# Opening of a one-core Perceiver kernel: spare products on TensorE, key weights split in three parts, and another order of TensorE's and ScalarE's first work

## The chip, the cores and the metric

The kernel runs on one core of a Trainium2 chip. A core has TensorE (PE in the profile: matmuls, with their weight loads listed apart as PEld), VectorE (DVE), ScalarE (ACT), GpSimd (POOL), SyncE (SP, which here only issues transfers) and 16 DMA engines. The engines run their own programs in order and meet through semaphores. The metric is the device time of one execution in microseconds (us), lower is better.

## The reference, cut to what matters

128 query rows of width 256 pass two layers. The change touches only the first operation of the first layer, a cross-attention over a context of 12544 rows with 16 heads, whose keys are 64 wide and whose values are 16 wide:

```python
q = (layernorm(x) @ wq)       # 128 x 1024, 16 heads of 64
k = (ctx @ wk)                # 12544 x 1024
v = (ctx @ wv)                # 12544 x 256, 16 heads of 16
attn = softmax(q @ k.T / sqrt(64), axis=-1)   # per head
x = x + attn @ v
```

After it come self-attention, a gated feed-forward, a second cross-attention, a causal self-attention and a mixture of experts. None of their code is changed.

## The kernel before, in words

**Tiles.** The context comes transposed, in chunks of 512 columns; the first one, the tail, has 256 (`TAIL_TILES` = 2). A chunk's keys are made in eight pairs of heads `p`. Context and key weights are each split into a high and a low part (`ctxT_hi`, `ctxT_lo`, `wk_hi`, `wk_lo`), and a pair's keys are six products, `TERMS` = 6, three for each half of the contraction (`key_term`, L361). The high part is a copy by ScalarE, the low part a subtraction by VectorE (weights) or GpSimd (context). Scores are made in eight steps `t`; a step takes 32 queries of a group of four pairs, so steps 0 to 3 need pairs 0 to 3 and the first half of the queries, steps 4 to 7 need pairs 4 to 7 and the second half (`scores`, L384). For each step VectorE takes the extreme value (`maxima`, L619), ScalarE the exponentials (`exponentials`, L554) followed by a drain that signals `scores_read`, VectorE transposes them (L638), and TensorE multiplies by the values (`weighted`, L394).

**The opening**, before the first call of `chunk`, is written out by hand, engine by engine. TensorE: the layer norm's transposes, then for each half of the heads: the queries (`queries`, L376; 8 matmuls, which the trace shows as 16 records, since a matmul of this type is recorded twice), a wait for the key weights of that half (`wk_split`), the tail's keys of four pairs in PSUM banks 4 and 5 alternately, and a wait for the scaled queries; after the first half also score steps 0 and 1. ScalarE: the context's high part, the copy of the normed x, the high part of the first 512 key weights columns (`wk_hi`, L581), the scaling of the queries (`keep_queries`, L548), four key copies (`keep_keys`, L544), the high parts of the second half of the key weights (L586) and of the value weights (L588), exponentials of step 0, second queries, key copies 4 and 5, exponentials of step 1, key copies 6 and 7, the next chunk's context (L540). VectorE takes the low parts of the key weights in two halves (L723) and of the value weights (L726), then the maxima.

**After it** comes `chunk(0, ...)`: score steps 2 and 3 of the tail, its values (L368), steps 4 and 5 (each waits until ScalarE has read the bank two steps before, `scores_read`), and the next chunk's keys. The first transfers are all issued at the start: x, the two halves of wq and the first full chunk by SyncE, the tail, the two halves of wk, and wv by ScalarE's queue.

**Spare products** (`spare_products`, L284) are matmuls of the identity with itself into a bank that nobody reads; the kernel has them already in the later stages, none in the opening.

Of the kernel before, what the change touches and what calls it, by code (L numbers as in the profile page):

```python
# [16 lines left out]
BANK = 512  # L17
# [5 lines left out]
TAIL_TILES = (N_KEYS // P) % CHUNK_TILES  # L23
# [257 lines left out]
def spare_products(pe, m, bank, count):  # L281

    for _ in range(count):
        pe.matmul(m.bank(bank)[:, 0:P], m.ident[:, :], m.ident[:, :], start=True, stop=True, skip_group_check=True)  # L284


def layer_norm_tensor(pe, m, s, n, bank):
    pe.wait_ge(s["xn_ready"], n("xn_ready"))
    for k in range(DK):
        t = pe.transpose(m.bank(bank)[:, k * P:(k + 1) * P], m.xn[:, k * P:(k + 1) * P], m.ident[:, :])  # L290
    t.then_inc(s["xnT_full"], 1)


def layer_norm_scalar(act, m, s, n, bank):
    act.wait_ge(s["xnT_full"], n("xnT_full"))
    act.copy(m.xnT[:, :, :], m.bank(bank)[:, 0:D].rearrange("p (k c) -> p k c", c=P)).then_inc(s["xnT_ready"], 1)
# [48 lines left out]


LAST_HALF, LAST_SUM = 3, 4


def per_head(t, f, u):  # L350
# [4 lines left out]
def xattn0_tensor(pe, m, s, n):  # L355
    def key_term(slot, p, nt, bank, i):

        k, term = divmod(i, 3)
        w = (m.wk_hi, m.wk_hi, m.wk_lo)[term]
        c = (m.c_hi, m.c_lo, m.c_hi)[term][slot]  # L360
        return pe.matmul(m.bank(bank)[:, 0:nt * P], w[:, k, p * P:(p + 1) * P], c[:, k, 0:nt * P],  # L361
                         start=(i == 0), stop=(i == TERMS - 1))
# [8 lines left out]
    def queries(half):  # L371
        pe.wait_ge(s[f"wq{half}"], 16)
        for i in range(4):
            p = 4 * half + i
            for k in range(DK):
                t = pe.matmul(m.bank(6 + half)[:, i * P:(i + 1) * P], m.wq[:, k, p * P:(p + 1) * P], m.xnT[:, k, :],  # L376
                              start=(k == 0), stop=(k == DK - 1))
        t.then_inc(s["q_full"], 1)

    def scores(slot, t, nt):  # L380
        group, qs = t // 4, slice(t % 4 * 32, t % 4 * 32 + 32)
        for j in range(4):
            for odd, rows in enumerate((TOP, LOW)):
                i = pe.matmul(m.ps[32 * j:32 * (j + 1), 2 * (t % 2) + odd, 0:nt * P], m.qT[rows, 4 * group + j, qs],  # L384
                              m.keys[slot][rows, 4 * group + j, 0:nt * P], start=True, stop=True,
                              skip_group_check=True)
        i.then_inc(s["scores_full"], 1)
# [115 lines left out]
        i.then_inc(s["last_turned"], 1)  # L503

    pe.wait_ge(s["ident"], 1)
    layer_norm_tensor(pe, m, s, n, 3)
    pe.wait_ge(s["xnT_ready"], n("xnT_ready"))
    for half in range(2):
        queries(half)
        if half == 0:  # L510
            pe.wait_ge(s["ctx_split"], n("ctx_split", 2))
            pe.sem_inc(s["raw_free"], 1)
        pe.wait_ge(s["wk_split"], n("wk_split"))
        for p in range(4 * half, 4 * half + 4):
            if p % 4 >= 2:
                pe.wait_ge(s["k_kept"], n("k_kept"))
            for i in range(TERMS):
                done = key_term(0, p, TAIL_TILES, 4 + p % 2, i)
            done.then_inc(s["k_full"], 1)
        pe.wait_ge(s["q_ready"], n("q_ready"))  # L520
        if half == 0:
            pe.wait_ge(s["k_kept"], n("k_kept", 2))
            for t in range(2):
                scores(0, t, TAIL_TILES)
    pe.wait_ge(s["wv_split"], n("wv_split"))
    chunk(0, TAIL_TILES, 0, 2)
    chunk(1, CHUNK_TILES, TAIL_TILES, 2)
# [8 lines left out]
def xattn0_scalar(act, m, s, n):  # L536
    def split_context(slot, k, nt):
        if k == 0:
            act.wait_ge(s[f"raw{slot}"], n(f"raw{slot}", 16))
        act.copy(m.c_hi[slot][:, k, 0:nt * P], m.raw[slot][:, k, 0:nt * P]).then_inc(s["ctx_hi"], 1)  # L540

    def keep_keys(slot, p, nt):
        act.wait_ge(s["k_full"], n("k_full"))
        act.copy(m.keys[slot][:, p, 0:nt * P], m.bank(4 + p % 2)[:, 0:nt * P]).then_inc(s["k_kept"], 1)  # L544

    def keep_queries(half):
        act.wait_ge(s["q_full"], n("q_full"))
        act.mul(m.qT[:, 4 * half:4 * half + 4, :], m.bank(6 + half).rearrange("p (h c) -> p h c", c=P),  # L548
                -float(X0_DK) ** -0.5).then_inc(s["q_ready"], 1)

    def exponentials(slot, t, nt, between=None):
        act.wait_ge(s["max_ready"], n("max_ready"))
        for odd in range(2):
            i = act.activation(m.probs[t % 2][:, odd, 0:nt * P], m.ps[:, 2 * (t % 2) + odd, 0:nt * P], ACT.Exp,  # L554
                               bias=m.peak[slot][:, 1, 2 * (t // 4) + odd, t % 4:t % 4 + 1], scale=-1.0,
                               accum_out=m.totals[slot][:, 1, 2 * (t // 4) + odd, t % 4:t % 4 + 1])
            if odd == 0 and between:
                keep_keys(*between, CHUNK_TILES)
        i.then_inc(s["probs_ready"], 1)
        act.drain().then_inc(s["scores_read"], 1)  # L560

    def chunk(slot, nt, ahead, first=False):
        for t in range(2 if first else 0, STEPS):
            keys = 1 - slot if t > 1 else slot
            kept = t < 2 or ahead
            exponentials(slot, t, nt, (keys, KEEP_BETWEEN[t]) if kept and t in KEEP_BETWEEN else None)
            if t == STEPS - 1:
                act.wait_ge(s["below_ready"], n("below_ready"))
                act.activation(m.shrink[slot][:, :, :, :], m.below[:, :, :, :],
                               ACT.Exp).then_inc(s["alpha_ready" if ahead else "alpha_last"], 1)  # L570
            if kept:
                for p in KEEP_AFTER.get(t, ()):
                    keep_keys(keys, p, CHUNK_TILES)
            if ahead > 1 and t in SPLIT_STEPS:
                split_context(slot, SPLIT_STEPS.index(t), CHUNK_TILES)

    for k in range(DK):
        split_context(0, k, TAIL_TILES)
    layer_norm_scalar(act, m, s, n, 3)
    act.wait_ge(s["wk0"], 16)  # L580
    act.copy(m.wk_hi[:, :, 0:BANK], m.wk[:, :, 0:BANK]).then_inc(s["wk_hi"], 1)  # L581
    keep_queries(0)
    for p in range(4):
        keep_keys(0, p, TAIL_TILES)
    act.wait_ge(s["wk1"], 16)
    act.copy(m.wk_hi[:, :, BANK:2 * BANK], m.wk[:, :, BANK:2 * BANK]).then_inc(s["wk_hi"], 1)  # L586
    act.wait_ge(s["wv"], 16)
    act.copy(m.wv_hi[:, :, :], m.wv[:, :, :]).then_inc(s["wv_hi"], 1)  # L588
    exponentials(0, 0, TAIL_TILES)
    keep_queries(1)  # L590
    for p in range(4, 6):
        keep_keys(0, p, TAIL_TILES)
    exponentials(0, 1, TAIL_TILES)
    for p in range(6, 8):
        keep_keys(0, p, TAIL_TILES)
    for k in range(DK):
        split_context(1, k, CHUNK_TILES)
    chunk(0, TAIL_TILES, 2, first=True)
    chunk(1, CHUNK_TILES, 2)
    looped = ("raw0", "raw1", "k_full", "max_ready", "below_ready")  # L600
    n.restart(act, s, *looped)
    with act.Fori(0, (N_FULL - 4) // 2):
        chunk(0, CHUNK_TILES, 2)
        chunk(1, CHUNK_TILES, 2)
        n.restart(act, s, *looped)
    chunk(0, CHUNK_TILES, 2)
    chunk(1, CHUNK_TILES, 1)
    chunk(0, CHUNK_TILES, 0)
    act.wait_ge(s["last_full"], 1)
    act.copy(m.last_out[0:64, :, :], m.ps[0:64, 6:8, 0:P]).then_inc(s["last_kept"], 1)  # L610
    act.wait_ge(s["last_full"], 2)
    act.copy(m.last_two[:, :, :], m.ps[:, 6:8, P:2 * P]).then_inc(s["last_kept"], 1)


def xattn0_vector(dv, m, s, n):
# [101 lines left out]

    dv.wait_ge(s["x"], 16)
    layer_norm_vector(dv, m, s, n, m.x[0][:, :])
    for half in range(2):  # L720
        cols = slice(half * BANK, (half + 1) * BANK)
        dv.wait_ge(s["wk_hi"], n("wk_hi"))
        dv.tensor_tensor(m.wk_lo[:, :, cols], m.wk[:, :, cols], m.wk_hi[:, :, cols],  # L723
                         ALU.subtract).then_inc(s["wk_split"], 1)
# [949 lines left out]
def build(nc, a, out):  # L1674
# [3 lines left out]
    with nc.Block() as block:  # L1678
        @block.tensor
        def tensor_program(pe):  # L1680
            n = Counts()
            xattn0_tensor(pe, m, s, n)
            attn0_tensor(pe, m, s, n)
            ffn0_tensor(pe, m, s, n)
            xattn1_tensor(pe, m, s, n)
            attn1_tensor(pe, m, s, n)
            moe_tensor(pe, m, s, n)
# [122 lines left out]
```

## Time and profile before

| | |
|---|---|
| time, median of 3 executions | 977.41 us (976.40 to 977.99) |
| time of the profiled execution | 980.61 us |
| its span in the trace | 978.0 us |
| TensorE busy | 951.1 us (97%) |
| VectorE, ScalarE, GpSimd busy | 71%, 60%, 38% |
| first cross-attention | from the start to about 650 us |
| opening, until the next chunk's keys start | 26.28 us |

The span runs from the first to the last instruction; 2.6 us of the profiled execution's time lie around it. Times in the trace are counted from the span's start. A matmul's end is modelled and neighbours overlap, so starts say more than ends.

### The profile page before, as it was taken

How to read it: one execution, taken by the hardware profiler on the slowest of the kernel's cores; microseconds unless marked ns; L12 is line 12 of the kernel's file. 1: busy time of each engine (PE TensorE's matmuls, PEld its weight loads, DVE VectorE, ACT ScalarE, POOL GpSimd, SP SyncE). 2: the span in 40 equal slices, each digit the busy share in tenths (PEclk: the TensorE clock that was granted, in tenths of full speed). 3: DMA queues.
4: the chain of work that ended last, by engine and by line, in shares of the span. 5: the costliest groups of instructions: out<-in, count | busy, mean ns of one | idle time of the engine just before them, and what ended most of it. 6: DMA issues, size and time to landing. Idle time of an engine off the chain costs nothing.

```text
span 978.0 us, 30798 instructions
## 1 busy us (share of the span) xinstructions
PE 951.1 (97%) x13287; PEld 703.0 (72%) x13287; DVE 689.9 (71%) x870; ACT 587.4 (60%) x1405; POOL 373.1 (38%) x407
## 2 busy tenths in 40 slices
PE   6999999999999999999999999988989999999998
PEld 6666666666666666666666666678978877789998
DVE  3788888888888888888888888763035654367886
ACT  5677766666666676666666666633246663336664
POOL 2344444444444444444444343331023334213332
PEclk9999999999999999999999999998999999999999
DMA  6100000100100001000100100049648988408992
GB/s 221 26 24 23 25 24 24 25 24 24 25 24 24 25 24 24 24 25 24 25 24 24 24 3 3 3 153 393 216 174 263 284 275 283 152 1 284 323 338 95
DMA packets 78296, 97.80 MB, mean 100 GB/s; under 512 B 21585, under 2 KB 56673, under 8 KB 78177
## 3 DMA queue, kind: packets, MB, share of 16 engines
q1 hardware_dynamic: 77088, 94.40, 29.9%
q8 instruction: 104, 1.70, 0.7%
q10 hardware_dynamic: 1088, 1.57, 0.4%
q14 instruction: 16, 0.12, 0.0%
HBM read 95.42 MB, written 0.13 MB: 98 GB/s over the span
## 4 chain that ended last, share of the span: by engine, by line
PE 89%; issue 4%; DVE 2%; POOL 2%; DMA 2%; ACT 1%; SPq 0%; ACTq 0%; DVEq 0%; POOLq 0%
PE ps L361 29%; PE ps L384 18%; PE ps L394 9%; PE ps L368 7%; PE ps L1508 6%; PE ps L1109 3%; PE ps L1010 3%; PE ps L1525 2%; PE ps L1529 2%; PE ps L1526 2%; PE ps L1098 1%; DMA m_shared_w<-in_m_sw 1%; PE ps L1100 1%; POOL m_w_lo L1490 1%; PE ps L1099 1%
## 5 line engine op out<-in xcount | busy, mean ns | idle before, releaser
L554 ACT ACTIVATE probs<-ps,x_peak 128x512 f32<-128x512 f32 (+1 forms) x400 | 269.6, 678 | 178.2 <-DVE x_peak L619 167.5
L619 DVE TENSOR_REDUCE x_peak<-ps 128x2 f32<-128x1024 f32 (+1 forms) x200 | 237.2, 1186 | 93.8 <-PE ps L384 93.8
L638 DVE STREAM_TRANSPOSE probsT<-probs 128x1024 f32<-128x1024 f32 (+1 forms) x200 | 242.9, 1215 | 13.2 <-ACT probs L554 12.6
L384 PE MATMUL ps<-keys,qT 64*32 64x512 f32 (+1 forms) x3200 | 195.7, 584 | 2.7 <-ACTq L560 1.6
L361 PE MATMUL ps<-ctxT_hi,wk_hi 128*128 128x512 f32 (+1 forms) x400 | 163.1, 408 | 0.8 <-ACT keys L544 0.8
L361 PE MATMUL ps<-ctxT_lo,wk_hi 128*128 128x512 f32 (+1 forms) x400 | 155.1, 388 | 0.0
L800 POOL TENSOR_SCALAR vals<-vals_t,x_side 128x512 f32<-128x512 f32 (+1 forms) x100 | 152.1, 1539 | 7.2 <-POOL x_totals L789 3.9
L361 PE MATMUL ps<-ctxT_hi,wk_lo 128*128 128x512 f32 (+1 forms) x400 | 154.1, 385 | 0.0
L361 PEld LDWEIGHTS ps<-ctxT_hi,wk_hi 128*128 128x128 f32 x400 | 75.3, 188 | 73.7 <-issue 39.8
L544 ACT COPY keys<-ps 128x512 f32<-128x512 f32 (+1 forms) x200 | 110.4, 577 | 28.7 <-PE ps L361 20.8
L766 POOL TENSOR_TENSOR ctxT_lo<-ctx_raw,ctxT_hi 128x512 fp32r<-128x512 f32 x48 | 61.6, 1284 | 134.7 <-ACT ctxT_hi L540 134.5
L384 PEld LDWEIGHTS ps<-keys,qT 64*32 64x32 f32 x3200 | 58.8, 106 | 70.6 <-issue 52.6
L394 PE MATMUL ps<-probsT,vals 64*32 64x128 f32 x6144 | 100.5, 271 | 0.0
L394 PEld LDWEIGHTS ps<-probsT,vals 64*32 64x32 f32 x6144 | 87.0, 105 | 18.2 <-issue 18.0
L361 PEld LDWEIGHTS ps<-ctxT_hi,wk_lo 128*128 128x128 f32 x400 | 75.6, 189 | 15.7
L361 PEld LDWEIGHTS ps<-ctxT_lo,wk_hi 128*128 128x128 f32 x400 | 75.7, 189 | 12.4
L554 ACT ACTIVATION_READ_ACCUMULATOR probs<-ps,x_peak 128x1 f32 x400 | 78.6, 197 | 0.0
L1290 POOL TENSOR_TENSOR c1T_lo<-ctx_two,c1T_hi 128x512 fp32r<-128x512 f32 (+1 forms) x25 | 31.3, 1251 | 93.4 <-ACT c1T_hi L1171 93.4
L783 POOL TENSOR_TENSOR x_parts<-x_totals,x_shrink 128x32 f32<-128x32 f32 x24 | 6.1, 253 | 158.6 <-DMA x_shrinkT<-x_shrink 158.6
L1480 POOL TENSOR_TENSOR m_w_lo<-m_w,m_w_hi 128x1024 fp32r<-128x1024 f32 x15 | 35.4, 2362 | 72.0 <-ACT m_w_hi L1557 72.0
L1508 PE MATMUL ps<-xnT,m_w 128*128 128x128 f32 x512 | 59.9, 275 | 0.0
L1508 PEld LDWEIGHTS ps<-xnT,m_w 128*128 128x128 f32 x512 | 58.6, 192 | 0.3 <-issue 0.3
(258 smaller groups left out, 1310.0 us busy)
## 6 DMA issues: line engine op xcount, KB each, us to landing
m_w<-in_m_w SPq DMA_DIRECT2D x32, 1024.0 KB, 7.8
ctx_raw<-in_ctxT SPq DMA_DIRECT2D x24, 512.0 KB, 3.7
ctx_two<-in_ctxT SPq DMA_DIRECT2D x24, 512.0 KB, 4.2
ctx_one<-in_ctx SPq DMA_DIRECT2D x24, 512.0 KB, 5.5
x_shrinkT<-x_shrink SPq DMA_DIRECT2D x384, 1.0 KB, 1.7
f_h1T<-in_f_h1T SPq DMA_DIRECT2D x1, 4096.0 KB, 18.5
f_h2T<-in_f_h2T SPq DMA_DIRECT2D x1, 4096.0 KB, 28.2
m_shared_w<-in_m_sw SPq DMA_DIRECT2D x2, 1024.0 KB, 8.9
```

What stands on the lines that cost most here:

```text
L361: return pe.matmul(m.bank(bank)[:, 0:nt * P], w[:, k, p * P:(p + 1) * P], c[:, k, 0:nt * P], start=(i == 0), stop=(i == TERMS - 1))
L368: return pe.matmul(m.bank(4 + half)[:, 0:nt * P], w[:, k, half * P:(half + 1) * P], c[:, k, 0:nt * P], start=(i == 0), stop=(i == TERMS - 1))
L384: i = pe.matmul(m.ps[32 * j:32 * (j + 1), 2 * (t % 2) + odd, 0:nt * P], m.qT[rows, 4 * group + j, qs], m.keys[slot][rows, 4 * group + j, 0 ...
L394: i = pe.matmul(m.ps[32 * c:32 * (c + 1), 6 + two, 0:P], m.vals[slot][rows, b, c, :], m.probsT[slot][rows, c, b, :], start=(b == 0), stop= ...
L544: act.copy(m.keys[slot][:, p, 0:nt * P], m.bank(4 + p % 2)[:, 0:nt * P]).then_inc(s["k_kept"], 1)
L554: i = act.activation(m.probs[t % 2][:, odd, 0:nt * P], m.ps[:, 2 * (t % 2) + odd, 0:nt * P], ACT.Exp, bias=m.peak[slot][:, 1, 2 * (t // 4) ...
L619: dv.tensor_reduce(m.peak[slot][:, 1, cs, t % 4], m.ps[:, 2 * (t % 2):2 * (t % 2) + 2, 0:nt * P], AX.X, ALU.min).then_inc(s["dve" if t == ...
L638: i = dv.transpose(m.probsT[slot][:, cs, 0:4 * nt, t % 4 * 32:t % 4 * 32 + 32], m.probs[t % 2][:, :, 0:nt * P].rearrange("p c (b k) -> p c ...
L766: gp.tensor_tensor(m.c_lo[slot][:, k, 0:nt * P], m.raw[slot][:, k, 0:nt * P], m.c_hi[slot][:, k, 0:nt * P], ALU.subtract).then_inc(s["ctx_ ...
L800: t = gp.tensor_scalar(m.vals[slot][:, 0:4 * nt, cs, side * X0_DV:(side + 1) * X0_DV], m.vals_t[slot][:, 0:4 * nt, cs, :], m.side[:, side: ...
L1480: eng.tensor_tensor(m.w2_lo[c % 2][:, os, :], second_weights(m, c)[:, os, :], m.w2_hi[c % 2][:, os, :], ALU.subtract).then_inc(s[f"m_w2_lo ...
L1508: t = pe.matmul(m.bank(2 * (c % 2) + half)[:, i * P:(i + 1) * P], w1[:, k, o * P:(o + 1) * P], m.xnT[:, k, :], start=(k == 0), stop=(k == ...
```

## The change: what it does

It edits the opening in four places. Seven spare products into bank 7 stand ahead of the layer norm's transposes, behind the wait for the identity. The key weights are split in three parts, columns 0 to 255, 256 to 511 and 512 to 1023, by ScalarE and VectorE alike, and TensorE waits for a part ahead of pairs 0, 2 and 4. TensorE makes the second half of the queries ahead of score steps 0 and 1, and its wait for the first scaled queries and for the four key copies moves with these. ScalarE splits the third part of the weights between key copies 1 and 2; it scales the second queries and copies key pair 4 ahead of the exponentials of step 0, and key pair 5 ahead of those of step 1.

```diff
+WK_PARTS = slice(0, BANK // 2), slice(BANK // 2, BANK), slice(BANK, 2 * BANK)
@@ xattn0_tensor
     pe.wait_ge(s["ident"], 1)
+    spare_products(pe, m, 7, 7)
     layer_norm_tensor(pe, m, s, n, 3)
     pe.wait_ge(s["xnT_ready"], n("xnT_ready"))
     for half in range(2):
...
         if half == 0:
             pe.wait_ge(s["ctx_split"], n("ctx_split", 2))
             pe.sem_inc(s["raw_free"], 1)
-        pe.wait_ge(s["wk_split"], n("wk_split"))
+        else:
+            pe.wait_ge(s["q_ready"], n("q_ready"))
+            pe.wait_ge(s["k_kept"], n("k_kept", 2))
+            for t in range(2):
+                scores(0, t, TAIL_TILES)
         for p in range(4 * half, 4 * half + 4):
+            if p in (0, 2, 4):
+                pe.wait_ge(s["wk_split"], n("wk_split"))
             if p % 4 >= 2:
                 pe.wait_ge(s["k_kept"], n("k_kept"))
             for i in range(TERMS):
                 done = key_term(0, p, TAIL_TILES, 4 + p % 2, i)
             done.then_inc(s["k_full"], 1)
-        pe.wait_ge(s["q_ready"], n("q_ready"))
-        if half == 0:
-            pe.wait_ge(s["k_kept"], n("k_kept", 2))
-            for t in range(2):
-                scores(0, t, TAIL_TILES)
+    pe.wait_ge(s["q_ready"], n("q_ready"))
     pe.wait_ge(s["wv_split"], n("wv_split"))
@@ xattn0_scalar
     act.wait_ge(s["wk0"], 16)
-    act.copy(m.wk_hi[:, :, 0:BANK], m.wk[:, :, 0:BANK]).then_inc(s["wk_hi"], 1)
+    for cols in WK_PARTS[0:2]:
+        act.copy(m.wk_hi[:, :, cols], m.wk[:, :, cols]).then_inc(s["wk_hi"], 1)
     keep_queries(0)
-    for p in range(4):
+    for p in range(2):
         keep_keys(0, p, TAIL_TILES)
     act.wait_ge(s["wk1"], 16)
-    act.copy(m.wk_hi[:, :, BANK:2 * BANK], m.wk[:, :, BANK:2 * BANK]).then_inc(s["wk_hi"], 1)
+    act.copy(m.wk_hi[:, :, WK_PARTS[2]], m.wk[:, :, WK_PARTS[2]]).then_inc(s["wk_hi"], 1)
+    for p in range(2, 4):
+        keep_keys(0, p, TAIL_TILES)
     act.wait_ge(s["wv"], 16)
     act.copy(m.wv_hi[:, :, :], m.wv[:, :, :]).then_inc(s["wv_hi"], 1)
+    keep_queries(1)
+    keep_keys(0, 4, TAIL_TILES)
     exponentials(0, 0, TAIL_TILES)
-    keep_queries(1)
-    for p in range(4, 6):
-        keep_keys(0, p, TAIL_TILES)
+    keep_keys(0, 5, TAIL_TILES)
     exponentials(0, 1, TAIL_TILES)
@@ xattn0_vector
-    for half in range(2):
-        cols = slice(half * BANK, (half + 1) * BANK)
+    for cols in WK_PARTS:
         dv.wait_ge(s["wk_hi"], n("wk_hi"))
         dv.tensor_tensor(m.wk_lo[:, :, cols], m.wk[:, :, cols], m.wk_hi[:, :, cols],
                          ALU.subtract).then_inc(s["wk_split"], 1)
```

## Rows read from the trace of the kernel before

**Rows 1.** The page: busy time, share of the span and instructions.

```profile
PE 951.1 (97%) x13287; PEld 703.0 (72%) x13287; DVE 689.9 (71%) x870; ACT 587.4 (60%) x1405; POOL 373.1 (38%) x407
```

**Rows 2.** Stretches: length, each engine's busy time, PEclk (granted clock), DMA share, GB/s.

```profile
0.00:26.28 26.28, 18.23 (x190) 15.21 (x190) 9.77 (x17) 13.85 (x35) 7.75 (x29) 1.00 0.59 206
26.28:649.75 623.47, 620.70 (x10752) 404.19 (x10752) 503.69 (x518) 417.69 (x1048) 276.56 (x314) 1.00 0.09 21
```

**Rows 3.** The chain that ended last, in the opening: start, us, what.

```profile
14.76 0.95 ACT wk_hi L586
```

**Rows 4.** Timeline of TensorE: start, us, engine line op, count, idle before and releaser.

```profile
5.43 0.66 PE L290 MATMUL ps<-ident,xn 128*128 128x128 f32 x2 [5.43 <-DVE xn L306]
6.82 3.75 PE L376 MATMUL ps<-xnT,x_wq 128*128 128x128 f32 x16 [0.73 <-DMA x_wq<-in_x_wq]
...
11.22 0.41 PE L361 MATMUL ps<-ctxT_hi,wk_hi 128*128 128x256 f32 x1
11.43 0.41 PE L361 MATMUL ps<-ctxT_lo,wk_hi 128*128 128x256 f32 x1
...
14.90 1.10 PE L384 MATMUL ps<-keys,qT 64*32 64x256 f32 x32 [0.56 <-ACT keys L544]
15.93 2.05 PE L376 MATMUL ps<-xnT,x_wq 128*128 128x128 f32 x16
17.74 0.36 PE L361 MATMUL ps<-ctxT_hi,wk_hi 128*128 128x256 f32 x1
...
25.69 0.67 PE L384 MATMUL ps<-keys,qT 64*32 64x256 f32 x16 [0.49 <-ACTq L560]
```

**Rows 5.** Timeline of ScalarE.

```profile
8.05 1.04 ACT L581 CAST wk_hi<-x_wk 128x1024 fp32r<-128x1024 f32 x1 [1.55 <-DMA x_wk<-in_x_wk]
...
12.10 0.37 ACT L544 COPY keys<-ps 128x256 f32<-128x256 f32 x1 [0.88 <-PE ps L361]
...
15.60 0.62 ACT L588 CAST wv_hi<-x_wv 128x512 fp32r<-128x512 f32 x1
18.20 0.47 ACT L554 ACTIVATE probs<-ps,x_peak 128x256 f32<-128x256 f32 x1 [1.98 <-DVE x_peak L619]
...
19.34 0.60 ACT L548 ACTIVATE qT<-ps 128x512 f32<-128x512 f32 x1
...
22.26 1.14 ACT L540 CAST ctxT_hi<-ctx_raw 128x512 fp32r<-128x512 f32 x2
23.38 0.47 ACT L554 ACTIVATE probs<-ps,x_peak 128x256 f32<-128x256 f32 x1
```

**Rows 6.** Timeline of VectorE.

```profile
9.13 1.23 DVE L723 TENSOR_TENSOR wk_lo<-x_wk,wk_hi 128x1024 fp32r<-128x1024 f32 x1 [3.84 <-ACT wk_hi L581]
...
16.88 0.68 DVE L726 TENSOR_TENSOR wv_lo<-x_wv,wv_hi 128x512 fp32r<-128x512 f32 x1
...
22.65 0.69 DVE L619 TENSOR_REDUCE x_peak<-ps 128x2 f32<-128x512 f32 x1 [2.69 <-PE ps L384]
```

**Rows 7.** Timeline of GpSimd.

```profile
1.90 0.29 POOL L323 TENSOR_SCALAR_AFFINE_SELECT ident<-ident 128x128 f32<-128x128 f32 x1
```

**Rows 8.** Instructions of the tiles x_wk and x_wv: issue of transfers, and their landing.

```profile
L879 ACTq DMA_DIRECT2D x_wk<-in_x_wk x2: 487/489/491, 1.3 to 1.8; - x2
...
DMA to landing us min/median/max: 6.8/7.9/9.0
...
L880 ACTq DMA_DIRECT2D x_wv<-in_x_wv x1: 640/640/640, 2.3 to 2.3; - x1
...
DMA to landing us min/median/max: 9.9/9.9/9.9
```

**Rows 9.** Stretches after the cross-attention; the third value from the right is PEclk.

```profile
671.00:672.00 1.00, 1.00 (x7) 1.00 (x6) 0.00 (x0) 0.00 (x0) 0.00 (x0) 0.50 0.99 397
...
677.00:678.00 1.00, 1.00 (x7) 1.00 (x7) 0.93 (x3) 0.00 (x0) 0.00 (x0) 0.58 1.08 362
...
729.00:730.00 1.00, 0.70 (x4) 0.46 (x3) 0.75 (x2) 0.18 (x1) 0.38 (x1) 0.99 0.98 382
```

## The prediction, made blind

> **What bounds the kernel now.** I read the page first: TensorE is busy 97% of the span [rows 1]. A table of stretches then shows where its idle time is. From 26.28 us to 649.75 us it is idle for 2.8 us in 623 [rows 2], with no wait to gain from. In the first 26.28 us it is busy for 18.23 us only, so 8.05 us are idle. The opening is the one place the edit touches, and what it saves there moves the long busy stretch forward as a whole. I take as the marker the first scores of step 5, at 25.69 us [rows 4]: behind them TensorE runs without a gap. The question is how much earlier they start.
>
> The timelines show what holds them back. TensorE is first needed at 5.43, has nothing until 6.82 (it waits for wq), and then works slowly: 16 query records take from 6.82 to 10.41, about 0.22 us each, where the same 16 take from 15.93 to 17.74 later, 0.11 each; key products are 0.21 us apart at 11.22 and 11.43 [rows 4], and, counting six of them behind the start at 17.74, 0.12 there. A ratio of two is the ratio of TensorE's two levels, 1.2 and 2.4 GHz. The granted clock is listed as 1.00 for the whole opening [rows 2], which the spacing contradicts, so I go by the spacing: the low level lasts until the spacing halves, at about 12.2 us. The chain of waits passes from TensorE's key products to ScalarE's split of the second half of wk at 14.76 [rows 3], then VectorE, then exponentials, and ScalarE is last to release step 5.
>
> **The change part by part.** I follow the new program from event to event.
>
> *Spare products.* The identity is written at 2.19 [rows 7]. Seven matmuls are 14 records; at the slow query spacing (3.59/16 = 0.224) that is 3.1 us, 2.25 to 5.4. The normed x is there at 5.43, so the transposes lose nothing, and if they lose 0.1 us, the wait for wq until 6.8 (0.73 us idle [rows 4]) covers it; beyond some 0.2 us the cover would be gone, and each further tenth would be a tenth of the path. What they buy is an earlier rise. Before the rise at 12.2 TensorE had been steadily busy since 6.82, 5.4 us. Elsewhere it runs at half, 0.50, at 671 and comes back within 677 to 678, and a second half-clock stretch ends by 729 to 730 [rows 9]. With spares, work begins at 2.25. By 5.4 us of work the rise comes at 7.7, or 8.5 if the 0.8 us gap ahead of the queries doesn't count. At 7.7 four query records are slow and twelve fast: 0.9 + 1.4, so they end at about 9.1; with 8.5 at about 9.5; with a rise ahead of them, at 8.6.
>
> *First key weights in two parts.* wk's first half is there at 8.05. A ScalarE split of 512 elements is 0.62 [rows 5], a VectorE one 0.68 [rows 6]. Part 0 is ready at 8.05 + 0.62 + 0.68 + 0.05 of handing over = 9.4, where the whole was ready at 10.36 (9.13 + 1.23). Part 1 follows at 10.0, ahead of pair 2, so its extra fixed cost is hidden. Key products start at 9.43, where they started at 10.41: this needs both the split and the faster queries. Four pairs of six at 0.12 take 2.87 us, to 12.3. Pair 2 needs key copy 0 (ScalarE: pair 0 done at 10.33, copy 0.37, 10.70) and begins at 10.86; pair 3 needs copy 1 at 11.42 and begins at 11.58. No stall, but margins of 0.15 us.
>
> *Other queries first.* Before, TensorE stood 0.56 us for key copy 3 ahead of the scores [rows 4]; now the queries (1.81 us) fill this: 12.3 to 14.1. Scores of steps 0 and 1 take 1.03 (14.90 to 15.93): to 15.13. Queries moved ahead pass no transfer; wq's second half is not awaited in the old trace.
>
> *Third part of wk.* ScalarE reaches it after copy 1, at 11.35. The transfer lands at 1.8 + 9.0 = 10.8 [rows 8], 0.5 us of slack. Split to 12.4, VectorE (1.23) to 13.65, needed at 15.13. Key copies 2 and 3 are queued behind it: done at 12.97, needed at 14.1. wv lands at 2.3 + 9.9 = 12.2 [rows 8], its split runs 12.9 to 13.5. All hidden; the chain's 0.95 us at 14.76 is gone from the path.
>
> *Copies ahead of exponentials.* Pairs 4 and 5 run 15.13 to 16.64 and their results need 0.15 more. The maxima of step 0 are ready at 14.7 + 0.7 [rows 6] = 15.4, but ScalarE stands until key 4 arrives: copy 16.1 to 16.45. This is the added wait: the exponentials, and scores steps 2 and 3 behind them, are queued behind it for 0.9 us. Exponentials of step 0 take 1.14 (18.20 to 19.34 [rows 5]): to 17.5; copy 5 to 17.85; step 1 to 19.0; copies 6 and 7 0.74, to 19.75. TensorE stands some 0.6 us ahead of pair 7, until 17.95, and ends it at 18.7, so its step 2 and 3 scores and values are behind ScalarE, not ahead.
>
> *The sum.* ScalarE's split of the next context, which began at 22.26 [rows 5], begins at 19.75: 2.5 us earlier. From here both programs are the same: two splits 1.12, exponentials 2 and 3 2.3, step 5 on TensorE at 23.15 instead of 25.69. GpSimd's low part of the context moves along. I take 0.1 off for narrow handovers: **2.4 us gained**. On the profiled execution that is 980.61 - 2.4 = 978.2; it lies 3.2 us above the median of the timed ones, so on their scale 977.41 - 2.4 = **975.0 us**.
>
> Bounds. Without any effect of the spares, key products start at 10.41 at slow spacing, end at 14.2, queries to 16.0, scores to 17.05, pair 4 done at 17.95, exponentials 18.3 to 19.4 and 19.7 to 20.9, copies to 21.6: 0.7 us gained by the new order alone. At the other end a rise ahead of the queries gains nothing over 9.43, since the split bounds that; dropping all my handovers gives 2.9.
>
> The row shows a rise 5.4 us after steady work began, and less elsewhere [rows 9]. The Trainium skill, "TensorE: Matmul & The Clock Gate", in its part on the HAM clock gate, says that the point of the rise depends on how the first matmul falls against a free-running counter, and warns not to fit a specific number of cold matmuls. By the trace alone the gain is 2.4 us; by that page the same kernel would give anything from 0.7 to 2.4 from one execution to the next. No run so far shows which.
>
> **The rivals.**
>
> *The spares don't bring the rise forward* (22%). The 0.8 us gap between transposes and queries may make the count start anew at 6.82, as before, and the rise comes at 12.2: 0.7 us gained, 976.7 us. For it: TensorE was also busy at 5.43, and that did not count then. Against: the gap is short beside the work around it. The page's rule named above would put executions in this case too, a reason for its chance.
>
> *Given back behind the opening* (10%). If some other chain, through VectorE's maxima or GpSimd's context split, holds step 5 or the next keys, the gain is lost: 977.4 us. For it: VectorE has 503.69 us of work in 623 [rows 2], with little to spare to catch up. Against: in the long stretch TensorE never waits for it longer than 2.8 us in total.
>
> *Slower: the clock falls in the new gaps* (8%). The new program leaves TensorE idle at 17.4 to 17.95, briefly ahead of the values, then 0.5 us ahead of steps 4 and 5 each, about 1.8 us in 5.7. The half-clock stretch from 671 to 677.4 [rows 9] lasted 6.4 us. A stretch of that length in the busy part costs half of it, 3.2 us: 0.8 us slower, 978.2 us. It decides from 4.8 us on, half of which is the gain. Against: before, gaps of 0.56, about 0.8 and 0.49 us within 11 us had no such effect.
>
> **How the numbers follow.** The forecast has 60%, with its own range 974.3 to 975.8 (a gain of 1.6 to 3.1). About 0.2% or 2.0 us is what a measurement of this kernel can tell from no change, and the forecast lies just beyond it: I give 48 of its 60 to faster and 12 to the same. The first rival, the second, and half of the third fall within 0.2%. A delay beyond 2 us has 4%, nearly all from a longer fall of the clock, and 1% from the forecast's lucky side of the others goes to faster. Faster 49%, same 47%, slower 4%. The range of eight in ten runs from 973.9 (the upper bound on the gain, and the timed median's own scatter) to 977.2, which takes in the first rival and leaves out the other two.
>
> **What would show it.** In the trace after: 14 records of L284 from 2.25; query records 0.11 apart by 9 us; the first L361 at about 9.4; no fall behind L586's successor; ScalarE waiting for TensorE ahead of key copy 4; the next chunk's ScalarE context split at 19.75; keys of 512 columns from 23.7, no gap behind. Wrong would be: query records 0.22 apart until 10.4, a transfer of wk's second half landing beyond 12.4, spacing doubled anywhere between 17 and 30 us, or a TensorE idle time beyond 3 us between 26 and 650.

## The result, and the profile after

Over 22 executions of each, the changed kernel took 979.76 us (977.98 to 983.89) where the one before took 977.32 us. The ratio is 1.003, with an interval of 1.002 to 1.004: **0.3% slower**, where 2.4 us had been predicted as a gain. The opening did get shorter. The loss lies behind it, in code that the edit doesn't touch.

The page after: the span, the row of busy times and the queue that carries instructions. The last columns of the queue are packets, megabytes and share of the DMA engines.

```profile
span 981.0 us, 30828 instructions
...
PE 956.9 (98%) x13301; PEld 705.4 (72%) x13301; DVE 689.8 (70%) x871; ACT 586.9 (60%) x1406; POOL 373.1 (38%) x407
...
q8 instruction: 105, 1.72, 0.7%
```

TensorE is busy 5.8 us longer than in [rows 1], with 14 matmuls and 14 weight loads more. A matmul shown as busy includes time in which it stands. Before, q8 carried 104 packets and 1.70 MB: 1.70 MB over the two times 13287 records of TensorE in [rows 1] is some 64 bytes for each record, so that each counts as one instruction, and a packet of 16.4 KB holds about 256 of them.

The stretches after, which answer to [rows 2]:

```profile
0.00:25.06 25.06, 20.60 (x205) 17.30 (x205) 9.97 (x18) 13.69 (x36) 7.74 (x29) 1.00 0.63 216
25.06:649.75 624.69, 622.31 (x10684) 402.80 (x10680) 501.65 (x514) 416.49 (x1046) 276.46 (x314) 1.00 0.09 21
```

The next chunk's keys start at 25.06, 1.22 us ahead of 26.28 before. TensorE's timeline of the opening after, beside [rows 4]:

```profile
2.24 3.36 PE L284 MATMUL ps<-ident 128*128 128x128 f32 x14 [2.24 <-POOL ident L323]
5.59 0.69 PE L290 MATMUL ps<-ident,xn 128*128 128x128 f32 x2
7.56 3.58 PE L377 MATMUL ps<-xnT,x_wq 128*128 128x128 f32 x16 [1.28 <-DMA x_wq<-in_x_wq]
10.90 0.37 PE L362 MATMUL ps<-ctxT_hi,wk_hi 128*128 128x256 f32 x1
11.10 0.28 PE L362 MATMUL ps<-ctxT_lo,wk_hi 128*128 128x256 f32 x1
...
13.92 1.95 PE L377 MATMUL ps<-xnT,x_wq 128*128 128x128 f32 x16
15.79 1.09 PE L385 MATMUL ps<-keys,qT 64*32 64x256 f32 x32
...
19.66 0.39 PE L362 MATMUL ps<-ctxT_hi,wk_hi 128*128 128x256 f32 x1 [0.43 <-ACT keys L548]
...
24.46 0.67 PE L385 MATMUL ps<-keys,qT 64*32 64x256 f32 x16 [0.47 <-ACTq L564]
```

The spare products stand where they should, and the queries behind them are still slow: 16 records in 3.34 us. Keys are 0.20 apart once and then 0.12, the spacing that the prediction read behind the rise: the clock rises at about 10.9, not at 7.7. Step 5 starts at 24.46, 1.23 us ahead of before. ScalarE's timeline after, beside [rows 5]:

```profile
7.93 1.14 ACT L586 CAST wk_hi<-x_wk 128x512 fp32r<-128x512 f32 x2 [1.25 <-DMA x_wk<-in_x_wk]
...
12.87 1.05 ACT L591 CAST wk_hi<-x_wk 128x1024 fp32r<-128x1024 f32 x1
...
17.83 0.37 ACT L548 COPY keys<-ps 128x256 f32<-128x256 f32 x1 [1.33 <-PE ps L362]
18.09 0.48 ACT L558 ACTIVATE probs<-ps,x_peak 128x256 f32<-128x256 f32 x1
...
21.17 1.15 ACT L544 CAST ctxT_hi<-ctx_raw 128x512 fp32r<-128x512 f32 x2
```

The parts of the weights land and are split without a wait on the path, the added wait ahead of key copy 4 is there (1.33 us), and the context's split comes 1.09 us earlier than before.

**Where it is given back.** In each chunk of the loop ScalarE makes `x_shrink` once, so its starts tell how long a chunk takes. Two of them, in the kernel before:

```profile
160.53 0.23 ACT L569 ACTIVATE x_shrink<-x_below 128x32 f32<-128x32 f32 x1
186.13 0.23 ACT L569 ACTIVATE x_shrink<-x_below 128x32 f32<-128x32 f32 x1
```

and the same two after:

```profile
159.33 0.23 ACT L573 ACTIVATE x_shrink<-x_below 128x32 f32<-128x32 f32 x1
185.97 0.23 ACT L573 ACTIVATE x_shrink<-x_below 128x32 f32<-128x32 f32 x1
```

Before, the chunk takes 25.60 us; after, 26.64. Behind the first two, nearly every chunk of either kernel takes 25.60. Five of the changed kernel take 26.64, 26.88, 26.54, 26.87 and 26.34, which is 5.3 us more in all. Before has one of 26.97, near the end of the stage, and its last takes 25.33 against 24.65. From the first mark to the 25th: 613.17 us before, 616.33 after, 3.16 lost.

TensorE's timeline shows the lost microsecond of the first late chunk, after:

```profile
157.81 2.03 PE L395 MATMUL ps<-probsT,vals 64*32 64x128 f32 x128
159.59 3.00 PE L385 MATMUL ps<-keys,qT 64*32 64x512 f32 x32
162.52 0.50 PE L362 MATMUL ps<-ctxT_hi,wk_hi 128*128 128x512 f32 x1
```

It is busy without a gap, yet the 32 score records take 2.93 us until the next product. At the same place of the changed kernel without its spare products (first experiment) they take 1.90:

```profile
157.77 2.03 PE L395 MATMUL ps<-probsT,vals 64*32 64x128 f32 x128
159.54 1.98 PE L385 MATMUL ps<-keys,qT 64*32 64x512 f32 x32
161.44 0.50 PE L362 MATMUL ps<-ctxT_hi,wk_hi 128*128 128x512 f32 x1
```

No releaser is named, and the records are the same in number. What falls there is the transfer of one packet of instructions. The transfers of 157 to 163 us after, each slice 0.15 us:

```profile
GB/s 0 0 0 0 0 0 0 0 0 0 0 0 109 0 0 0 0 0 0 0 0 0 0 0 0 7 0 0 0 6 1 0 0 5 3 0 0 3 4 0
...
q8 instruction: 1, 0.02, 1.3%
```

The packet starts at 157 + 12 x 0.15 = 158.8, and 1.3% of 16 engines' 6 us is 1.25 us for it. The values and scores around it are 160 short records, with as many weight loads, which TensorE works off in 3.7 us. In the changed kernel without its spare products, where nothing stands, the packet starts one slice later:

```profile
GB/s 0 0 0 0 0 0 0 0 0 0 0 0 0 109 0 0 0 0 0 0 0 0 0 0 3 4 0 0 1 6 0 0 0 7 1 0 0 5 2 0
...
q8 instruction: 1, 0.02, 1.1%
```

Between two marks of the loop TensorE has 888 recorded instructions, and in two chunks, 400 to 451.2 us, q8 carries seven packets in either kernel. A chunk is thus 3.5 packets, so its code comes back to the same place against them in every second chunk.

**The end of the stage** loses nearly as much again. TensorE's timeline after:

```profile
645.11 1.09 PE L385 MATMUL ps<-keys,qT 64*32 64x512 f32 x16 [1.17 <-ACTq L564]
646.64 3.70 PE L395 MATMUL ps<-probsT,vals 64*32 64x128 f32 x128 [0.44 <-issue]
...
651.36 1.73 PE L489 MATMUL ps<-probsT,vals 64*32 64x128 f32 x103 [0.25 <-DVE probsT L645]
654.04 0.64 PE L489 MATMUL ps<-probsT,vals 64*32 64x128 f32 x25 [0.95 <-issue]
...
656.52 5.15 PE L284 MATMUL ps<-ident 128*128 128x128 f32 x32
```

and before:

```profile
643.18 1.09 PE L384 MATMUL ps<-keys,qT 64*32 64x512 f32 x16 [1.12 <-ACTq L560]
644.06 3.67 PE L394 MATMUL ps<-probsT,vals 64*32 64x128 f32 x128
...
649.43 2.18 PE L488 MATMUL ps<-probsT,vals 64*32 64x128 f32 x128 [0.93 <-DVE probsT L638]
...
653.18 3.79 PE L284 MATMUL ps<-ident 128*128 128x128 f32 x32
```

After, "issue" cuts into a run of 128 equal records (103 and 25), with 0.95 us in which TensorE waits for nothing that the profile shows. Behind it the next stage's spare products, 32 records, take 5.15 us instead of 3.79. The stretches after say why (third value from the right is the granted clock):

```profile
655.00:656.00 1.00, 0.83 (x6) 0.76 (x7) 0.73 (x4) 0.12 (x1) 0.00 (x0) 0.97 1.14 397
656.00:660.00 4.00, 4.00 (x23) 4.00 (x23) 2.40 (x7) 0.00 (x0) 0.69 (x2) 0.58 0.95 346
660.00:661.00 1.00, 1.00 (x11) 1.00 (x11) 0.00 (x0) 0.00 (x0) 0.00 (x0) 1.00 1.02 422
```

For most of four microseconds the clock is at the lower of its two levels, 1.2 GHz. From the 25th mark to the next stage's first product behind its spare ones it is 12.41 us after and 9.65 before.

**The sum of the two profiled executions:** opening -1.23, first to 25th mark +3.16, from there to the next stage +2.76, the rest -1.71 (before had a half-clock stretch at 848 to 852 us that the execution after lacked). Together +3.0, the two spans' difference; the medians differ by 2.4.

### The profile page after: what moved, and what is told of

Same layout as the page of the kernel before. It is cut to its first block, busy times and chain, and to the rows that moved or that the text cites. A ratio compares the mean times of both kernels' runs of the same rounds, so it can differ in the third digit from the quotient of the medians.

```text
span 981.0 us, 30828 instructions
## 1 busy us (share of the span) xinstructions
PE 956.9 (98%) x13301; PEld 705.4 (72%) x13301; DVE 689.8 (70%) x871; ACT 586.9 (60%) x1406; POOL 373.1 (38%) x407
## 4 chain that ended last, share of the span: by engine, by line
PE 89%; issue 3%; DVE 2%; POOL 2%; DMA 2%; ACT 1%; SPq 0%; ACTq 0%; DVEq 0%; POOLq 0%
PE ps L362 29%; PE ps L385 18%; PE ps L395 9%; PE ps L369 7%; PE ps L1514 6%; PE ps L1115 3%; PE ps L1016 3%; PE ps L1531 2%; PE ps L1535 2%; PE ps L1532 2%; PE ps L1104 1%; DMA m_shared_w<-in_m_sw 1%; POOL m_w_lo L1496 1%; PE ps L1106 1%; PE ps L1105 1%
## 5 line engine op out<-in xcount | busy, mean ns | idle before, releaser
L385 PE MATMUL ps<-keys,qT 64*32 64x512 f32 (+1 forms) x3200 | 198.3, 584 | 2.5 <-ACTq L564 1.9
L362 PEld LDWEIGHTS ps<-ctxT_lo,wk_hi 128*128 128x128 f32 x400 | 75.2, 188 | 12.4
```

## The experiments

The theories. **A, the place of the code:** the seven spare products put 28 more instructions of TensorE (14 matmuls, 14 loads) ahead of the loop. Its code then stands otherwise against the packets of 256, and, by the theory, one packet in every second chunk comes too late for a run of short products. **The rivals:** the new order brings back its gain later, through another engine's lateness; the spare products' early work makes the clock fall elsewhere (not in the loop, where the stretch from 25.06 to 649.75 us has 1.00); or the profiled executions differ by chance. Only A says that what counts is the number of instructions ahead of the loop, modulo 256, whatever they do.

Each kernel was compared with the one before, on the same chip. Late chunks are those of 25.75 us or more among the first 20 of the 24 intervals between marks. All kernels with none of them, one_wide apart, have a single one of 26.4 to 27.0 in the 22nd or 23rd interval instead. It is not counted as late, but it is in the time from the first to the 25th mark.

| kernel | instructions added ahead of the loop by products or increments | ratio, interval | step 5 starts | late chunks | 1st to 25th mark | 25th mark to next stage |
|---|---|---|---|---|---|---|
| before | 0 | 1 | 25.69 | 0 | 613.17 | 9.65 |
| after | 28 | 1.003 (1.002 to 1.004) | 24.46 | 5 | 616.33 | 12.41 |
| no_spares | 0 | 0.9989 (0.9978 to 1.0) | 24.44 | 0 | 612.50 | 9.47 |
| order_only | 0 | 1.0008 (0.999 to 1.0026) | 24.36 | 0 | 612.33 | 9.47 |
| spares_only | 28 | 1.0036 (1.0023 to 1.0049) | 24.64 | 5 | 614.56 | 13.01 |
| pad_only | 28 | 1.0049 (1.0032 to 1.0066) | 26.50 | 4 | 614.34 | 10.79 |
| before_plus_256 | 256 | 1.0027 (1.0014 to 1.004) | 27.92 | 0 | 612.62 | 9.64 |
| before_plus_128 | 128 | 1.0005 (0.9989 to 1.002) | 25.25 | 0 | 612.26 | 11.05 |
| after_plus_256 | 256 | 1.002 (1.0004 to 1.0035) | 27.11 | 0 | 612.18 | 9.64 |
| after_plus_224 | 224 | 1.0066 (1.0042 to 1.009) | 26.17 | 5 | 616.15 | 12.50 |
| wide_spares | 8 | 0.9992 (0.9973 to 1.001) | 22.79 | 2 | 612.06 | 11.94 |
| one_wide | 4 | 0.9989 (0.9976 to 1.0002) | 24.35 | 0 | 611.36 | 11.89 |
| wide_and_small | 60 | 1.0002 (0.9987 to 1.0016) | 24.27 | 0 | 613.23 | 9.46 |

### One half of the change at a time: no_spares and spares_only

no_spares is the changed kernel less one line; spares_only is the kernel before with that line.

```diff
     pe.wait_ge(s["ident"], 1)
-    spare_products(pe, m, 7, 7)
```

> The changed kernel without its seven spare products; all the rest of the change stays. Theory A (place of the code: the 28 more TensorE instructions ahead of the loop move the loop's code against the blocks in which instructions are fetched, and a block then comes late for the short score products once an iteration): no extra 1 us in the loop's chunks, which take 25.60 us each again; the opening gives about 0.7 us; total 0.5 to 1.5 us under before, ratio 0.9985 to 0.9995. Theory B (the new order of the opening puts the engines in another phase, whose waits return in every iteration): the chunks of 26.3 to 26.9 us stay, total 2 to 3 us over before, ratio 1.002 to 1.003. Theory C (the spare products' load on the clock later): as A in the total, but no late chunk in the after trace would have been at full clock.

> The kernel before with the seven spare products ahead of the layer norm and nothing else of the change. Theory A: chunks of 26.3 to 26.9 us come up in the loop as in the changed kernel (0 to 10 of them), 2 to 4 us over before less up to 0.8 us of earlier clock: ratio 1.002 to 1.004. Theory B: loop chunks all 25.60 us, total 0 to 0.8 us under before, ratio 0.999 to 1.000.

The loss follows the spare products, in either company. Without them: no late chunk in the loop, 0.9989. Alone: five late chunks, 1.0036. The order and the parts are thus worth about -0.1% and the spare products +0.4%, and both together 1.003. The rival that blames the new order is out. In the loop spares_only loses 1.4 us by the marks and at the stage's end 3.4, so the end carries more of its loss than the late chunks do. It showed one thing more: its clock had risen by 6.8 us.

```profile
2.25 3.35 PE L284 MATMUL ps<-ident 128*128 128x128 f32 x14 [2.25 <-POOL ident L323]
5.49 0.69 PE L290 MATMUL ps<-ident,xn 128*128 128x128 f32 x2
6.64 2.09 PE L376 MATMUL ps<-xnT,x_wq 128*128 128x128 f32 x16 [0.46 <-ACT xnT L296]
10.19 0.39 PE L361 MATMUL ps<-ctxT_hi,wk_hi 128*128 128x256 f32 x1 [1.45 <-DVE wk_lo L724]
```

Here TensorE then waits 1.45 us for the undivided key weights, which is why the prediction wanted parts and faster queries together; the start of step 5 at 24.64 is a gain of 1.05 from the faster clock.

### The same number of instructions, with no products: pad_only

```diff
     pe.wait_ge(s["ident"], 1)
+    for _ in range(28):
+        pe.sem_inc(s["ident"], 1)
```

> The kernel before with 28 semaphore increments on TensorE's queue ahead of the layer norm, on a semaphore that nobody waits for again: as many instructions as seven spare products are, and no work for the array; they run while TensorE waits for the normed x. Theory A: same late chunks as in the changed kernel, 1 to 4 us over before, ratio 1.001 to 1.004. Theory B and a theory by which the products' own activity is to blame: no change, ratio 0.9995 to 1.0005.

The kernel before with 28 instructions that only raise a semaphore. They cost TensorE its place in the opening (transposes at 6.49 instead of 5.43, step 5 0.81 us later), which explains a sixth of the 4.8 us lost. By the marks the loop loses another 1.2 us and the stage's end 1.1; behind them this profiled execution was faster than that of before, so the rest of the 4.8 stays without a place. (1.001 to 1.004 had been expected.) The late chunks are back, without one product added:

```profile
161.38 0.23 ACT L571 ACTIVATE x_shrink<-x_below 128x32 f32<-128x32 f32 x1
187.48 0.23 ACT L571 ACTIVATE x_shrink<-x_below 128x32 f32<-128x32 f32 x1
```

26.10 here, and 26.55, 26.66 and 26.34 later; a further one of 25.64 is hardly late. Neither spare products nor an early clock is needed for the loss.

### A whole packet more: before_plus_256, after_plus_256, after_plus_224

Products of 32 columns by 64 rows, a matmul and a load recorded twice each: 64 of them are 256 instructions, 56 are 224. (The kernels have them in a helper; it is written out here.)

```diff
+    for _ in range(64):
+        pe.matmul(m.ps[0:32, 7, 0:32], m.ident[0:64, 0:32], m.ident[0:64, 0:32],
+                  start=True, stop=True, skip_group_check=True)
```

> The kernel before with 64 very small products (32 by 32, 64 rows) ahead of the layer norm, 256 instructions: exactly one 16 KB packet of the instruction queue at 64 bytes each, so that the loop's code keeps its place against the packets. Theory A (place of the code): no late chunk in the loop, all 25.60 us, though nine times as many instructions were added as in the run with 28; total within 1.5 us of before, ratio 0.998 to 1.001. Theory A2 (any more instructions ahead of the loop delay it): late chunks, 2 us or more over before, ratio over 1.002.

> The changed kernel with 64 small products, one whole packet. Theory A: no late chunks, the loop as without spare products; the transposes 0.5 us late at most, hidden by the wait for wq; 1 to 3 us under before, ratio 0.997 to 0.999. Theory A2: over 1.002.

> The changed kernel with 56 small products in place of the seven spare ones, 224 instructions, 32 short of a packet: the borders fall 32 instructions later in the loop than before, on the long key products. Theory A: no late chunks in the loop; the opening gains at least 1.2 us, 2.5 if the small products raise the clock: 1 to 3 us under before, ratio 0.997 to 0.999. Theory A2: over 1.002.

I had taken the small products for nearly hidden. They are not:

```profile
2.24 7.03 PE L284 MATMUL ps<-ident 64*32 64x32 f32 x128 [2.24 <-POOL ident L330]
```

0.055 us a record, 7.03 us until 9.3, so step 5 comes 2.23 us later than before, and the ratio (1.0027, 2.6 us, where 0.998 to 1.001 was expected) is that within its interval. None of its chunks counts as late. The same 64 in the changed kernel, in place of its spare products, take away its five late chunks. The one between its sixth and seventh marks:

```profile
161.98 0.23 ACT L580 ACTIVATE x_shrink<-x_below 128x32 f32<-128x32 f32 x1
187.58 0.23 ACT L580 ACTIVATE x_shrink<-x_below 128x32 f32<-128x32 f32 x1
```

It takes 25.60 us, where the changed kernel took 26.64. From the first to the 25th mark the run takes 612.18 us, against 616.33. Giving the changed kernel 228 instructions more (256 for 28) takes 4 us from the code behind them. The ratio is still 1.002, not the 0.997 to 0.999 expected: step 5 starts 1.42 us later than before.

A clean loop alone doesn't show that 256 counts as 0, since 4, 60 and 128 give one too. The finer pattern does more for it. All five kernels with 0 or 256, with either order of the opening, have their one long chunk (26.43 to 26.97) in the 23rd interval and 9.47 to 9.65 us from the 25th mark to the next stage. Of the other counts none has both: 60 and 128 have it in the 22nd, 4 has none, 8, 28 and 224 have theirs far earlier. A whole packet more brings back the same pattern, although step 5 then starts 1.4 and 2.2 us later than before, and in no_spares and order_only 1.3 us sooner; so it isn't the shift in time that counts. This is the strongest evidence for A.

With 224, which is 32 short of a packet, I had expected a clean loop and was wrong: five late chunks, 616.15 us from the first to the 25th mark, 1.0066. Modulo 256, both 28 too many and 32 too few are bad places, and 0 is a good one. That fits A as a place, but not my picture of one narrow bad spot just behind the good one.

### Other places: before_plus_128, wide_and_small

before_plus_128 has 32 small products. wide_and_small has one wide product (below) and 14 small ones, in the changed kernel.

> As the last, with 32 small products, 128 instructions: half a packet. Theory A: a pattern of its own, other than that of 0 and 256; late chunks where a packet's border falls so that a whole packet lies in the burst of short products. Which sign can't be worked out from the rows; anything from no late chunk to one of 1 us in each loop iteration (10 us), ratio 0.999 to 1.010. Theory A2: 2 us or more over before as with 28 and with 256.

> The changed kernel with one spare product of 512 columns and 14 small ones in place of the seven: 60 instructions, 3.4 us. Place theory: the packets' border falls 60 instructions earlier than before and 32 earlier than in the changed kernel, so inside the weighted products ahead of the scores; a shift between the bad one of 28 and the good one of 128. Late chunks in the loop if the border is still in the burst: 2 to 8, ratio 1.001 to 1.004; if it is through, none, ratio 0.997 to 0.999.

Neither has a late chunk (612.26 and 613.23 us from the first to the 25th mark), and neither is faster than before; for wide_and_small without late chunks 0.997 to 0.999 had been expected. Places 0, 4, 60 and 128 are good, 28 and -32 bad, and 8 in part (next). before_plus_128 loses at the end of the stage (11.05), so that part has a pattern of its own.

### The spare work in fewer instructions: wide_spares, one_wide

A product of 512 columns keeps TensorE busy as long as four of 128 (0.85 us a record against 0.21), with a fourth of the instructions.

```diff
-    spare_products(pe, m, 7, 7)
+    for _ in range(2):          # one_wide: 1
+        pe.matmul(m.bank(7).rearrange("p (r c) -> p r c", c=P), m.ident[:, :],
+                  m.ident[:, :].unsqueeze(1).to_broadcast([P, 4, P]),
+                  start=True, stop=True, skip_group_check=True)
```

> The changed kernel with two spare products of 512 columns in place of seven of 128: as much array time (about 3.4 us at the low level), 8 instructions instead of 28. Theory A: the loop's code lies only 8 instructions from its place before, so few or no late chunks; the opening as in the changed kernel (1.2 us) or better: 1 to 2.5 us under before, ratio 0.9975 to 0.999. Theory B: late chunks stay, ratio 1.002 to 1.003.

> The changed kernel with one spare product of 512 columns (4 instructions, about 1.9 us) in place of the seven. Place theory: with 4 instructions of shift 0 to 2 late chunks. TensorE idles some 1.3 us between spare and transposes, so the clock rises as without spares or earlier. 0.5 to 2 us under before, ratio 0.998 to 0.9995. If place has nothing to do with it, ratio over 1.001.

wide_spares shows the opening as the prediction drew it:

```profile
2.24 3.78 PE L284 MATMUL ps<-ident 128*128 128x512 f32 x4 [2.24 <-POOL ident L330]
...
6.92 2.54 PE L384 MATMUL ps<-xnT,x_wq 128*128 128x128 f32 x16 [0.46 <-ACT xnT L303]
9.21 0.37 PE L369 MATMUL ps<-ctxT_hi,wk_hi 128*128 128x256 f32 x1
...
22.79 0.67 PE L392 MATMUL ps<-keys,qT 64*32 64x256 f32 x16 [0.47 <-ACTq L571]
```

Keys start at 9.21 (9.43 forecast) and step 5 at 22.79 (23.15 forecast): 2.9 us gained in the opening, with the rise at about 8.0. Over its 12 executions the kernel is at 0.9992 only. Two chunks are late (26.34 and 25.79), and the end of the stage has stalls of 1.76 and 1.19 us put down to "issue". one_wide, at place 4, has no late chunk, and its clock rose late, at 11.45: 0.9989. Its stage's end is as long as that of wide_spares (11.89, with a stall of 2.07).

### The order alone: order_only

no_spares with the key weights in two halves again, so that only TensorE's and ScalarE's order differs from before.

```diff
-WK_PARTS = slice(0, BANK // 2), slice(BANK // 2, BANK), slice(BANK, 2 * BANK)
+WK_PARTS = slice(0, BANK), slice(BANK, 2 * BANK)
...
-            if p in (0, 2, 4):
+            if p in (0, 4):
...
```

> The changed kernel without spare products and with the key weights in two halves again, as before: only the new order of the work is left. By my blind reckoning of the late rise the order alone gives 0.7 us: step 5 of the scores at 24.7 to 25.0. The run without spare products and with three parts had it at 24.44. If the split in parts is worth something with a late rise, this one is later than that by up to 0.6 us; if queries end it anyway, equal. No late chunks but those behind the loop. Ratio 0.9985 to 1.000.

Step 5 starts at 24.36, as in no_spares (24.44). Against before that is 1.33 us by the order alone, and the parts add nothing in these two profiled executions, in which the clock rose late: the keys of order_only start right behind the queries, with no wait for the weights. The two differ elsewhere too: order_only began its queries 0.5 us sooner, and its clock rose 0.6 us later (12.0 against 11.4). The ratio, 1.0008 (0.999 to 1.0026), is not the gain that I had expected (0.9985 to 1.000), and its interval holds both no change and the 0.1% of no_spares.

### The changed kernel once more: after_again

> The changed kernel once more, unedited, for one look. The place theory: late chunks of 26.3 to 26.9 us again (3 to 8), the stalls inside the short score products, and a late block again inside the last chunk's products. On the clock: if the point of its rise is set by something that the program doesn't set, spacing halves at another time than the 10.9 us of the first look, anywhere from 6 to 11, and step 5 starts at 22.8 to 24.5 accordingly; if the program sets it, at 10.9 and 24.46 again.

```profile
6.94 3.75 PE L377 MATMUL ps<-xnT,x_wq 128*128 128x128 f32 x16 [0.91 <-DMA x_wq<-in_x_wq]
...
24.34 0.67 PE L385 MATMUL ps<-keys,qT 64*32 64x256 f32 x16 [0.47 <-ACTq L564]
```

The one execution took 980.15 us. The queries are slow again (rise at about 11.3), with wq there 0.6 us sooner. The five late chunks are in the same intervals as in the first profiled execution, with 26.62, 26.13, 26.60, 26.67 and 26.56, and the stage's end takes 11.74. They belong to the program, not to chance.

## Why the prediction was wrong, point by point

**The step that failed** is in the prediction's first paragraph: what the edit saves in the opening "moves the long busy stretch forward as a whole". "From here both programs are the same" says it again. The operations are the same. Their place in TensorE's stream of instructions is not, since the spare products are 28 instructions ahead of some 21,500 in the long stretch. I counted their time and their records and not where they push the rest. The stretch did not move as a whole: it starts 1.2 us sooner, and in the profiled executions the loop and the stage's end take 3.16 and 2.76 us more. By the ratios the spare products cost some 4 us (1.003 against 0.9989 without them). No rival held this: the second, which gives the gain back behind the opening, stops at no change, and the slower one is about the clock in the new gaps. **A term was mis-sized too**, the rise of the clock (below): the opening gained 1.23 us and not 2.4.

**That second rival** was about a chain through VectorE's maxima or GpSimd's split. None of them is late. Its bound, the 2.8 us that TensorE is idle in the long stretch, was no bound on such a loss: a product that stands is listed as busy (159.59, 3.00 us), and behind 25.06 us TensorE is idle for 624.69 - 622.31 = 2.4 us, less than before.

**The slower rival** did not occur: there is no half-speed spacing between 17 and 30 us. A fall of the clock did come, 640 us later, behind the stalls of the stage's end, and costs about 1.4 of the 2.76 us there (5.15 against 3.79). Its price was read a little short: with 0.58 in 677 to 678 [rows 9] the half-clock stretch ends at about 677.8, not 677.4.

**The rise of the clock.** "By 5.4 us of work the rise comes at 7.7" did not hold. It came at 10.9 and 11.3 in the two profiled executions of the changed kernel, at 11.4 without spares, at 11.45 with one wide product. It came by 6.8 in spares_only and at 8.0 in wide_spares, and at 13.3 in pad_only. Small products did not hasten it: with 3.6 us of them it came at 11.3, with 7.0 us at 13.1 and 13.3. So the first rival (0.7 us, 22%) is what both profiled executions of the changed kernel show. Of the four with 3 us and more of spare products of 128 or 512 columns alone two rose early, of the others none; so few give no rate. The Trainium skill, "TensorE: Matmul & The Clock Gate", in its part on the HAM clock gate, has the point of the rise depend on a free-running counter. The scatter fits that, though no run shows the counter; it is wider than the 0.5 us either way that the page names, since behind the same seven spare products the rise came by 6.8 and at 10.9.

**The new order.** "0.7 us gained by the new order alone" was mis-sized: 1.25 us in no_spares and 1.33 in order_only. I had the exponentials of step 0 at 18.3, of step 1 at 19.7 and the copies done at 21.6; they came at 18.09, at 19.50 and by 21.2, a few tenths sooner each. With the rise early, the whole opening gained 2.9 (wide_spares) against 2.4. One profiled execution stands behind each of these numbers.

**Right:** the key weights' parts in time, the fill of the 0.56 us gap by the queries, the added wait ahead of key copy 4 and the stand of some 0.6 us ahead of pair 7 (0.43).

**What stays open.** The changed kernel's late chunks come from the sixth to the fourteenth interval, in every second one, and not in the rest of the loop, which has the same code; why not, no run tells. The packets do creep along the code: in the kernel before one starts 9.0 us behind the mark in the third interval and 12.4 in the 23rd. Nor is it shown whether and how a packet's transfer turns into the stand of the scores: its start was read from slices of 0.15 us, and a packet that starts one slice later does no harm. What the runs show is that the number of instructions ahead decides. Which places are bad could not be foretold, as 224 showed. The stage's end has its own pattern (9.5 to 13.0 us), which was not varied alone. Setting the loop's start to a fixed place by other means was not tried. And no version beats the one before by more than its interval: no_spares and one_wide, both 0.9989, come nearest, and both beat the changed kernel by 0.4%.

## What to carry to other kernels

An instruction added ahead of a long run of short matmuls moves all of it against the packets in which code is fetched, and that can cost more than its own time. Count the instructions, not only the time. Filler work in few and wide products cost less here (0.9992 and 0.9989 against 1.003), though 4 and 8 instructions still made the stage's end 2.3 us longer. When a kernel gets slower in code that was not edited, measure the length of one iteration from a mark that occurs once in it, look at the long ones, and test by adding or replacing instructions up to a whole packet. An idle time near zero doesn't exclude stalls, since a standing matmul is drawn as busy.

## What the runs showed of the hardware

- **Instruction packets of TensorE.** 28 instructions ahead of the loop cost 3.5 us of 977 as products (spares_only) and 4.8 as semaphore increments (pad_only, 0.8 of it in the opening); 256 cost 2.6, within the interval no more than the 2.2 of their own time. The Trainium skill, "Advanced Engine Details and Errata", section "ISA Cache", gives lines of 16 KB, 256 instructions; q8's 16.4 KB a packet and the pattern that comes back with 256 agree. The Trainium skill, "Runtime: NRT & Kernel Launch", section "Instruction fetch mechanics", calls the cost of a border mostly hidden. Against that stand late chunks longer by 0.2 to 1.4 us each, in the same intervals in both profiled executions of the changed kernel.
- **Small products are not free.** One of 64 rows by 32 columns took 0.055 us a record at the start of the kernel, 7.03 us for 128.
- **The granted clock is no witness in the opening.** It reads 1.00 for 0.00 to 25.06 us, while 16 query records take 3.34 us from 7.56 on and the 16 of the second half take 1.87 us from 13.92 on.
- **Landing times scatter.** wq ended TensorE's wait at 7.56 in one execution of the changed kernel and at 6.94 in the next.
